# Weighted values split into two halves, their sum by source in one-pass products, in the slots that also have edge scores

## The reference, cut to what matters

```
x  = layernorm(x + gnn_and_lstm(x, adj))
Xq = (H @ W_lin.T).reshape(bt, n, h, dh);  Xv = (H @ W_val.T).reshape(bt, n, h, dh)
e  = einsum('behd,hd->beh', leaky_relu(Xq[:, src] + Xq[:, dst], 0.2), a) + log(A0[src, dst] + EPS)
attn = softmax of e over the edges with the same src
Y  = segment_sum(attn[..., None] * Xv[:, dst], src)      # the sum by source
out = layernorm(x + Y @ W_out.T)
```

## Time and profile before

| | |
|---|---|
| median of 3 runs | 921.08 us |
| profiled execution | 919.82 us |
| its span | 918.0 us, granted clock 0.993 |
| PE busy | 876.0 us |
| DVE, ACT, POOL busy | 694.4, 613.0, 174.2 us |
| sum by source (L1133), matmuls | 512 records, 63.5 us busy |

### The profile page before, as it was taken

How to read it: one execution, slowest core, us unless ns; L and a number is a source line. 1 busy time by engine, 2 the same in 40 slices (tenths; PEclk the granted TensorE clock), 3 DMA queues, 4 the chain that set the end, 5 groups by cost and what they waited for, 6 DMA issues and landing times.

```text
span 918.0 us, 15431 instructions
## 1 busy us (share of the span) xinstructions
PE 876.0 (95%) x5411; PEld 760.3 (83%) x5411; DVE 694.4 (76%) x1560; ACT 613.0 (67%) x1116; POOL 174.2 (19%) x509
## 2 busy tenths in 40 slices
PE   7999999999999999999999999999999999998884
PEld 6888888877787789999998887877887888886774
DVE  5777777777778777778777767677786887886874
ACT  2677777777676766766676666666786777764344
POOL 0000000000000000000000000003653654656665
PEclk9999999999999999999999999999999999999998
DMA  4212111001000000000000276783550011111112
GB/s 111 80 47 65 56 54 46 24 1 46 1 1 1 0 1 1 1 2 1 1 1 1 47 166 155 173 187 99 100 132 1 25 35 36 36 36 41 47 53 69
DMA packets 43260, 45.44 MB, mean 50 GB/s; under 512 B 2576, under 2 KB 40112, under 8 KB 40112
## 3 DMA queue, kind: packets, MB, share of 16 engines
q1 hardware_dynamic: 39504, 27.47, 10.5%
q0 software_dynamic: 2304, 16.78, 9.0%
q10 hardware_dynamic: 1376, 0.22, 0.2%
HBM read 19.29 MB, written 8.39 MB: 30 GB/s over the span
## 4 chain that ended last, share of the span: by engine, by line
PE 75%; DVE 8%; DMA 6%; issue 5%; ACT 3%; POOL 2%; ACTq 0%; DVEq 0%; POOLq 0%
PE psum L443 7%; PE psum L444 7%; PE psum L445 7%; PE psum L1060 6%; PE psum L461 5%; PE psum L457 5%; PE psum L1133 5%; PE psum L458 5%; DMA hT_lo<-x_stage 3%; PE psum L361 3%; PE psum L379 3%; PE psum L389 3%; PE psum L1144 2%; PE psum L352 2%; PE psum L351 2%
## 5 line engine op out<-in xcount | busy, mean ns | idle before, releaser
L559 ACT ACTIVATE work<-psum,bias 128x512 f32<-128x512 f32 (+1 forms) x408 | 233.6, 622 | 30.0 <-PE psum L461 29.4
L443 PE MATMUL psum<-hT_hi,w_hi 128*128 128x512 f32 (+1 forms) x408 | 148.7, 364 | 3.3 <-ACT work L559 2.6
L444 PE MATMUL psum<-hT_lo,w_hi 128*128 128x512 f32 (+1 forms) x408 | 147.2, 361 | 0.0
L445 PE MATMUL psum<-hT_hi,w_lo 128*128 128x512 f32 (+1 forms) x408 | 147.1, 361 | 0.0
L545 ACT ACTIVATE work<-work 128x512 f32<-128x512 f32 (+1 forms) x112 | 63.8, 570 | 103.9 <-DVE work L811 72.5
L971 POOL DMA_DIRECT2D hT_lo<-hT_hi x8 | 7.3, 916 | 556.5 <-DVE hT_lo L786 537.3
L818 DVE TENSOR_TENSOR work<-work 128x512 f32<-128x512 f32 (+1 forms) x112 | 68.5, 612 | 55.2 <-ACT work L545 55.2
L457 PE MATMUL psum<-hs_hi,w_hi 128*128 128x512 f32 (+1 forms) x288 | 103.9, 361 | 1.5 <-DVE hs_hi L784 1.4
L461 PE MATMUL psum<-hs_lo,w_hi 128*128 128x512 f32 (+1 forms) x288 | 104.4, 362 | 0.0
L458 PE MATMUL psum<-hs_hi,w_lo 128*128 128x512 f32 (+1 forms) x288 | 103.1, 358 | 0.0
L443 PEld LDWEIGHTS psum<-hT_hi,w_hi 128*128 128x128 f32 x408 | 76.8, 188 | 17.4 <-ACT work L559 5.4
(11 more groups left out here) (191 smaller groups left out, 1876.4 us busy)
## 6 DMA issues: line engine op xcount, KB each, us to landing
work<-x SPq DMA_DIRECT2D x32, 256.0 KB, 3.0
x_stage<-x_by_feature SPq DMA_DIRECT2D x8, 1024.0 KB, 5.6
hT_lo<-hT_hi POOLq DMA_DIRECT2D x8, 1024.0 KB, 9.6
hT_lo<-x_stage POOLq DMA_DIRECT2D x8, 1024.0 KB, 7.0
out<-x_kept SPq DMA_DIRECT2D x32, 256.0 KB, 2.3
work<-L_gnn_Wih SPq DMA_DIRECT2D x4, 256.0 KB, 3.0
work<-L_gnn_Whh SPq DMA_DIRECT2D x3, 256.0 KB, 3.0
bg_all<-L_gnn_bg ACTq DMA_DIRECT2D x2, 64.0 KB, 5.1
```

The lines of the kernel that those rows point to most:

```text
L443: pe.matmul(out, w_hi[:, w, g, :], xh, start=True, stop=False)
L444: pe.matmul(out, w_hi[:, w, g, :], xl, start=False, stop=False)
L445: mm = pe.matmul(out, w_lo[:, w, g, :], xh, start=False, stop=(t == 0))
L559: op = act.activation(gate[s][g][:, 0:ph.width], psum[:, 4 * s + g, 0:ph.width], ACT.Tanh if g == G else ACT.Sigmoid, bias=bias[:, b:b + 1])
```

## The change

For the tiles 0 to 19 the weighted values are split. ACT copies each half of `va` into `va_hi` in float32r (`weighted_hi`), POOL subtracts that from `va` into `va_lo` (`value_lo(k, c)` of `run_gpsimd`; DVE's `value_lo(k)` is another), and PE makes the sum by source with two float32r products for each float32 product. The late tiles keep the float32 products. `va` has one buffer now, which pays, with two tiles less in the ring, for `va_hi` and `va_lo`. PE has `edge_scores` and `turn` ahead of the sum by source, and DVE has `stats_in` ahead of the first `weight_values`.

```diff
-        self.from_node = sb("from_node", [P, EC, P])
+        self.from_node = sb("from_node", [P, EC, P], F32R)
...
-    RING = LAG + 9
+    RING = LAG + 7
...
-    va = sb("va", [P, 2, EC, TW])
+    va, va_hi, va_lo = sb("va", [P, EC, TW]), sb("va_hi", [P, EC, TW], F32R), sb("va_lo", [P, EC, TW], F32R)
...
+        def value_lo(k, c):
+            pool.wait_ge(S["va_hi_ready"], EC * k + c + 1)
+            pool.tensor_tensor(va_lo[:, c], va[:, c], va_hi[:, c].bitcast(F32), SUB).then_inc(S["va_split"], 1)
...
             if has(n + 2) or has(n - 2 - LAG):
                 factors(n)
+            if has(n - LAG) and not late(n - LAG):
+                for c in range(EC):
+                    value_lo(n - LAG, c)
...
         def sum_by_source(k):
-            pe.wait_ge(S["va_ready"], EC * (k + 1))
+            if late(k):
+                pe.wait_ge(S["va_ready"], EC * (k + 1))
+            else:
+                pe.wait_ge(S["va_split"], EC * (k + 1))
...
             for b in range(BT):
+                cols = slice(b * P, (b + 1) * P)
                 for c in range(EC):
...
+                    else:
+                        pe.matmul(psum[:, sum_bank(k), cols], va_hi[:, c, cols], from_node[:, c, :], start=(c == 0), stop=False)
+                        mm = pe.matmul(psum[:, sum_bank(k), cols], va_lo[:, c, cols], from_node[:, c, :], start=False, stop=(c == EC - 1))
             mm.then_inc(S["yt_psum"], 1)
...
+            if has(n - 1):
+                edge_scores(n - 1)
+            if has(n + 2):
+                turn(n + 2)
             if has(n - 1 - LAG):
                 sum_by_source(n - 1 - LAG)
-            if has(n - 1):
-                edge_scores(n - 1)
             if has(n - LAG):
                 value_gather(n - LAG, 0)
-            if has(n + 2):
-                turn(n + 2)
...
+        def weighted_hi(k, c):
+            act.wait_ge(S["va_ready"], EC * k + c + 1)
+            if k:
+                act.wait_ge(S["yt_psum"], k)
+            act.activation(va_hi[:, c], va[:, c], ACT.Copy).then_inc(S["va_hi_ready"], 1)
...
-            if has(n):
-                leaky_relu(n, 0)
-                leaky_relu(n, 1)
+            for h in range(EC):
+                if has(n):
+                    leaky_relu(n, h)
+                if has(n - LAG) and not late(n - LAG):
+                    weighted_hi(n - LAG, h)
...
-            if k >= 2:
-                dve.wait_ge(S["yt_psum"], k - 1)
+            if k and late(k):
+                dve.wait_ge(S["yt_psum"], k)
+            elif k:
+                dve.wait_ge(S["va_split"], EC * (k - 1) + c + 1)
...
+            if has(n + 2):
+                stats_in(n + 2)
             if has(n - LAG):
                 weight_values(n - LAG, 0)
-            if has(n + 2):
-                stats_in(n + 2)
             if has(n - LAG):
                 weight_values(n - LAG, 1)
```

More of the change, by code:

```diff
@@ L879, in back @@
              "z_psum leaky_ready edges_psum log_added max_f max_b below_max exp_done sum_f sum_b recip_done attn_row attn_psum "
-             "edge_rstd_ready attn_ready vg_psum va_ready yt_psum yT_ready o_psum o_read stats2_done "
+             "edge_rstd_ready attn_ready vg_psum va_ready va_hi_ready va_split yt_psum yT_ready o_psum o_read stats2_done "
              "halves scaled squared var_done rstd_done factors_done out_act out_pool")
@@ L1131, in sum_by_source @@
             for b in range(BT):
+                cols = slice(b * P, (b + 1) * P)
                 for c in range(EC):
-                    mm = pe.matmul(psum[:, sum_bank(k), b * P:(b + 1) * P], va[:, k % 2, c, b * P:(b + 1) * P], from_node[:, c, :],
-                                   start=(c == 0), stop=(c == EC - 1))
+                    if late(k):
+                        mm = pe.matmul(psum[:, sum_bank(k), cols], va[:, c, cols], from_node[:, c, :].bitcast(F32), start=(c == 0), stop=(c == EC - 1))
+                    else:
+                        pe.matmul(psum[:, sum_bank(k), cols], va_hi[:, c, cols], from_node[:, c, :], start=(c == 0), stop=False)
+                        mm = pe.matmul(psum[:, sum_bank(k), cols], va_lo[:, c, cols], from_node[:, c, :], start=False, stop=(c == EC - 1))
             mm.then_inc(S["yt_psum"], 1)
@@ L1347, in weight_values @@
             dve.wait_ge(S["vg_psum"], EC * k + c + 1)
-            if k >= 2:
-                dve.wait_ge(S["yt_psum"], k - 1)
+            if k and late(k):
+                dve.wait_ge(S["yt_psum"], k)
+            elif k:
+                dve.wait_ge(S["va_split"], EC * (k - 1) + c + 1)
             w = attn[:, g % 2, c, :].rearrange("p (b r) -> p b r", b=BT)[:, :, n * HEADS:(n + 1) * HEADS]
-            dve.tensor_tensor(va[:, k % 2, c, :].rearrange("p (b h d) -> p b h d", b=BT, d=DH),
+            dve.tensor_tensor(va[:, c, :].rearrange("p (b h d) -> p b h d", b=BT, d=DH),
                               psum[:, gather_bank(k, c), :].rearrange("p (b h d) -> p b h d", b=BT, d=DH),
```

## The result

The changed kernel takes 971.33 us (median of 4 runs, 969.34 to 973.27) against 920.85 for the kernel before on the same chip: ratio 1.0549, 95% interval 1.0531 to 1.0568. The forecast was 967. The profiled execution took 969.34 us, span 967.5.

The account below looks back on a forecast made before the run. PE bound the kernel at 7.75 us a slot; a ring of 10.86 us would replace it. Delay of 48.1 us by sum(16), 46.4 after exit and shorter products, on 919.82 gave 966; forecast 967, range 945 to 996.

Parts of the forecast that it names:

- Products: PE's sum by source: 16 load-bound one-pass products at 0.110 us, 1.76 against 1.79 us per tile, 0.6 us over 20 tiles.
- The ring: Each sum by source waits for the one before through all five engines' queues: 10.86 us a round against 7.75.
- L: Length of one 128x512 va_lo subtraction on POOL, taken as 1.3 us; each 0.1 costs 3.4 us in all.
- The balance: Delays of the sums by source: 48.1 us by sum(16), +47.0 by sum(19), 46.4 with 0.6 off for shorter products.
- entry: First sums of the changed tiles: sum(0) 2.7 us late, sum(1) 9.55 us after it.
- exit: From slot 30 the ring is open: delay falls from +48.1 us at sum(17) to +47.0 at sum(19).
- Rival 4: Clock falls to 1.2 GHz as PE idles; PE's work from 7.7 to some 13 us, 1001 us; chance 0.03.
- Rivals 1 to 3: Dear POOL subtraction, 997 us, chance 0.11; cheap one, 946, 0.08; ring not closing, 919 or 902, 0.06.
- rival 1: POOL's subtraction dear, 2.0 us or more, by its two inputs or DVE at the port; 997 us; chance 0.11.
- Moving turn ahead of the sum does not help: On PE, turn's place ahead of the sum by source gains nothing, as read_turned follows copy_yT on ACT.
- the 2.0 us before the second value_gather: PE idle per slot, as DVE has stats_in ahead of the first weight_values and the single VG bank holds PE.

Follow-up runs that it names:

- e7: Changed kernel without the va_lo products in tiles 0 to 19, 8 products a tile instead of 16; 958.13 us.
- e12: Changed kernel with the split and its waits kept, but PE multiplying the float32 va in all tiles; 969.18 us.
- e8: Changed kernel with a third subtraction on POOL per tile, the second half of va_lo written twice; 997.95 us.
- e1: Changed kernel with the two va_lo subtractions ahead of factors on POOL; 982.65 us.
- e9: e3 with ACT's normalize_out moved to the end of its slot, behind the copies to va_hi; 926.62 us.
- e2: Changed kernel with stats_in put back between the two weight_values on DVE; 980.23 us.
- e5: Changed kernel with PE's old order: sum, edge scores, first value_gather, turn; 999.46 us.
- e4: Kernel before, without the split, with the changed kernel's order on PE and on DVE; 959.32 us.
- e3: Changed kernel with both va_lo subtractions ahead of factors on POOL and stats_in between the two weight_values on DVE; 953.72 us.
- e6: Kernel before, without the split, with the changed kernel's order on PE alone; 926.58 us.
- e11: e4 with six unused float32 products filling PE's idle time before the second value_gather in slots 13 to 29; 950.31 us.

## Why the prediction was right, and where it was not

**Products.** It took 110 ns a product. 112 were measured, e7 gave 0.11, and e12 gave 0.04 us a round between one-pass and float32 products, where 0.03 had been taken. There was nothing to win. That the load is the bound rests on the earlier trace rows, 113 ns for a stream of only 32 columns; no run here shortened the stream alone. By the Trainium skill's rule (TensorE: Matmul & The Clock Gate, LDWEIGHTS) a load of 128 columns takes 107 ns, and the 110 to 113 ns of the traces are near it; the 81 ns of the same page (Back-to-back issue gap) are in none.

**The ring.** Its pieces as predicted and as measured in the round from 790.45: sum to copy_yT 2.15 and 2.04; to read_turned 0.50 and 0.49; to stats_in 0.64 and 0.63; to factors 0.95 and 0.95; factors, the gap behind it and the two subtractions 3.91 + 0.11 + 2.6 = 6.62, and 801.00 - 794.56 = 6.44. Sum 10.86 and 10.55. The 0.3 are gaps counted too wide (the first subtraction starts before the record of shift ends) and L = 1.3 for what is 1.25 in a pair. e8 shows that POOL is in it one for one. That the order on POOL closes it is shown by e1's one round of 9.60 and, with the other two rings open as well, by the 8.22 of e9. The estimate of 1.3 us for a subtraction, worked out from the 2.6 cycles per element of the Trainium skill (GPSIMD Engine Reference, elementwise cycle accounting), agrees with the 1.28 of the trace.

**The balance** of the profiled runs, in starts of sums: entry +2.5 predicted as 2.7 (sum 0); 1.88 for sum 1, predicted 1.8; 42.4 for the 15 rounds, predicted 43.7; exit -0.7, predicted -1.1 (sum 19). Two terms were not in the sum: 2.0 us ahead of the changed slots, of which 1.6 fall where a stretch at 1.2 GHz lasts longer in this run (mean clock from 640.00 to 646.80: 0.78 before, 0.51 after), and 1.4 at sum 20, where another falls. Together 49.5, the growth of the span. The forecast's rounds were 0.3 too long and had no lowered clock in them, and these two errors partly cancel: 162.9 against 161.56. The mechanism was right; that the total came so near is in part luck.

**Rival 4**, the clock, was a cause in small: four of 15 rounds, 3.3 us. The row that spoke against it was one short stretch. In e1, e2, e5, e7 and e8 more of the rounds were disturbed. The price of this rival, some 13 us for PE's work, came from no row: where the clock was at 1.2 GHz, output's 8 products took 1.91 us instead of 1.05 (e4), and in no run did it stay there for all of the rounds. Rivals 1 to 3 did not come about: L is neither 2.0 nor 0.68, and the ring closed. The mechanism of rival 1, DVE slowing POOL, exists (e2), but was seen only beside a scan, and not for every instruction there.

**What failed.** "Moving turn ahead of the sum does not help: read_turned stands behind copy_yT on ACT anyway" is wrong: e5 shows 1.19 us a round. copy_yT waits only for the sum, and the turn would come behind the scores and the first value_gather. And the 2.0 us before the second value_gather were told as idle time inside the ring, not as a ring of its own that closes at 9.65 us (e4). To open POOL's alone gives 0.95 us at best (one round of e1), and e1 as a whole was slower than the changed kernel: the orders of POOL, DVE and ACT all have to be undone (e9). Nor did the prediction, or the expectations of e1 and e3, see the third ring through normalize_out (e9).

**Open.** How much of e1's and e2's excess is the clock and how much the third ring or the scans was not separated by a run; none of either had PE's idle time filled. The smaller RING and the single buffer of `va` were not tried by themselves either, but e9, which has them, has the same rounds of 8.22 us as e6, which has not. normalize_out last in its slot, in the kernel before and without a split, was not tried, though e9's late tiles suggest some 4 us. No kernel run here beat the one before.

## What to carry to other kernels

When a wait is moved behind another piece of work in a queue, follow the chain from it back through every engine's order until it meets itself; if it does, the sum of that chain is the new period, whatever the busy shares say. Look for all such rings, since the one beneath the longest decides what undoing it brings. And two one-pass products in place of one float32 product gave nothing here, since the loads and matmuls stay 16 a tile at 0.11 us each; leaving eight of them out gave 0.9 us (e7).

## What the hardware showed that I had not expected

- With PE idle once or twice a round (1.78 and 0.69 us of 10.55 in the changed kernel, 1.82 of 9.65 in e4) the granted clock fell to 1.2 GHz in some rounds and not in others; filling the 1.8 us kept it at 2.4 and made the kernel 9 us faster (e11 against e4).
- A scan on DVE (0.68 us) held a POOL instruction of 0.25 us for 0.73 (e2), and a pair of subtractions for 0.38 us longer. `rstd`, with a scan of 0.72 us beside it in the changed kernel, took its usual 1.67 us. It goes the other way too: in e3 a scan that began (726.00) beside a running subtraction took 1.50 us instead of 0.68.
- The same reordering of PE gained 1.19 us a round inside one ring (changed kernel against e5) and lost 0.47 outside it (e6 against before).
